# A state-space mixer with a routed expert layer: VectorE's routing through PSUM, another head and tail, and the expert tiles four units apart

## The chip, the cores and the metric

One core of a Trainium2 chip runs the whole program. The metric is the device time of one execution in microseconds. The kernel before took 2276.89 us in the median of three runs (2268.54 to 2281.24).

## What is computed

There are 16 sequences ("batches" below) of 512 tokens with 512 channels, all float32:

```
xn = layernorm(x)
x_dbl = xn @ x_proj_w.T                    # 128 + 16 (B) + 16 (C) columns
delta = softplus(x_dbl[:, :128] @ dt_proj_w.T + dt_proj_b)
state[d,n] = exp(delta[d] * A[d,n]) * state[d,n] + delta[d] * B[n] * xn[d]   # along the 512 tokens
s[d] = sum over n of state[d,n] * C[n] + xn[d] * D[d]                        # n = 0..15
top = the 2 best of 8 experts by xn @ gate_w + gate_b
f = mean over the two of relu(xn @ expert_w[e] + expert_b[e])
out = x + s * silu(f)
```

## The kernel before

**Units.** Channels lie on the 128 partitions, in four blocks (`dt`), and each of the 16 states `n` of a block is one unit: 64 units for a batch, called 0 to 63 here. A unit is one recurrence over 512 tokens. ScalarE makes the decay (`da_unit`, exp into one of three PSUM banks of `scan_ps`), GpSimd the input term for two units at once (`dbx_pair`, up to four pairs ahead), and VectorE runs the recurrence as one scan (`scan`). Then the state is multiplied by C: in most units by VectorE (`times_c`, into `p_sb`), in the last one or two units of a quad (four units) by GpSimd two quads later (`times_c_quad`, from `h_sb` into `pp_sb`). `POOL_C` says how many of a quad are GpSimd's; it is 20 of 64 in a batch. TensorE transposes each product and sums it in `y_ps` (`add_y`, `add_y_quad`), and ScalarE copies the sum of a channel block to `s_sb` (`copy_y`).

**The expert layer.** VectorE picks two experts for each token (`gate`) and works out a row for each of the 1024 choices, so that rows of one expert are together (`rank`). GpSimd scatters the tokens to those rows in DRAM (`scatter`), in 15 tiles of 128 rows. For each tile TensorE transposes the rows (`turn_rows`), multiplies by the weights of the tile's expert (`tile`), and ScalarE copies and rectifies (`keep_turned`, `tile_relu`). GpSimd gathers both rows of each token into `acc` with two indirect transfers (`gather_first`, `gather_second`, the second one adding). ScalarE then makes the sigmoid in three steps (`sigmoid`) and VectorE the output (`combine`), for the batch before, while the next one is being scanned.

**Order.** Each engine's order is written out: every engine runs the 64 units in turn, and tables say at which unit's place another piece of work stands. `STEPS` holds TensorE's projection steps (NT transposes xn, NX projects and gates, NK counts rows, NR and NS turn the results, Z0 to Z3 make delta; N is for the next batch); ScalarE follows `COPY_LAG` units later. `TILE_AT` holds the tiles, `SIG_AT` and `OUT_AT` sigmoid and combine, `FIRST_AT`, `SECOND_AT` and `SCATTER_AT` the quads at which GpSimd issues its indirect transfers. ScalarE stands at most three units ahead of VectorE, because it waits until a bank of `scan_ps` is free. Batches 0, 1, 14 and 15 are written out; a hardware loop of six turns does two batches a turn.

Of the kernel before, what the change touches and what calls it, by code (L numbers as in the profile page):

```python
# [54 lines left out]
FIRST_ROWS_AT = (5, 6)  # L55


def build(nc, x, xw, dw, db, alog, dpar, gw, gb, ew, eb, out):
# [14 lines left out]
    ND = [QUAD - c for c in POOL_C]  # L73
    DVE_C = sum(ND)

    ctx = ExitStack()
    with ctx:
# [45 lines left out]
        pool_pad = sb("pool_pad", [P, 5])  # L123
# [74 lines left out]
        row_sum = sem("row_sum")  # L198
        own_ready = sem("own_ready")
# [29 lines left out]

        def step_no(b, name):  # L230
# [21 lines left out]
        def quad_no(b, q):  # L252
            return b * QUADS + q
# [23 lines left out]
        def _(sp):  # L277
# [873 lines left out]
```

## Time and profile before

| | |
|---|---|
| median of three runs | 2276.89 us |
| the profiled execution | 2277.99 us, span 2276.2 us |
| VectorE busy | 1983.9 us, 87% |
| GpSimd busy | 1888.0 us, 83% |
| TensorE busy (matmul) | 1843.6 us, 81%; mean granted clock 0.93 of 2.4 GHz |
| ScalarE busy | 1378.6 us, 61% |
| transfers | 641 MB, 282 GB/s |

The profile was taken on one execution. A row of the order of time gives start, duration, engine, line, operation, output<-inputs and shape; in brackets how long the engine had been idle and what ended that. A row on waits gives who waited for whom, the total, how often, and the longest. PE is TensorE, DVE VectorE, ACT ScalarE, POOL GpSimd. Where several instructions of a kind stand in a row, they are one row with a count.

### The profile page before, as it was taken

How to read it: one execution, taken by the hardware profiler on the slowest of the kernel's cores; microseconds unless marked ns; L12 is line 12 of the kernel's file. 1: busy time of each engine (PE TensorE's matmuls, PEld its weight loads, DVE VectorE, ACT ScalarE, POOL GpSimd, SP SyncE). 2: the span in 40 equal slices, each digit the busy share in tenths (PEclk: the TensorE clock that was granted, in tenths of full speed). 3: DMA queues.
4: the chain of work that ended last, by engine and by line, in shares of the span. 5: the costliest groups of instructions: out<-in, count | busy, mean ns of one | idle time of the engine just before them, and what ended most of it. 6: DMA issues, size and time to landing. Idle time of an engine off the chain costs nothing.

```text
span 2276.2 us, 35000 instructions
## 1 busy us (share of the span) xinstructions
PE 1843.6 (81%) x8688; PEld 1192.7 (52%) x8688; DVE 1983.9 (87%) x3002; ACT 1378.6 (61%) x2370; POOL 1888.0 (83%) x1146
## 2 busy tenths in 40 slices
PE   2597988979788797888969888797987979888883
PEld 2364655546455564555546555465654646565552
DVE  3688898999889998899988989899888999989985
ACT  2465666666476665666656576565665666566663
POOL 2679889888888988889888988789888898898993
PEclk8698999989899998998989999899998999999997
DMA  5868798788968878798887978789797897987974
GB/s 212 291 229 336 238 345 279 266 323 256 365 199 308 310 259 327 232 327 290 262 309 240 367 245 295 278 258 367 222 323 258 267 352 228 360 269 265 337 253 127
DMA packets 281729, 641.47 MB, mean 282 GB/s; under 512 B 22529, under 2 KB 23041, under 8 KB 273297
## 3 DMA queue, kind: packets, MB, share of 16 engines
q1 hardware_dynamic: 187792, 445.84, 55.2%
q10 hardware_dynamic: 69120, 125.86, 15.6%
q0 software_dynamic: 24576, 67.13, 10.6%
q8 instruction: 83, 1.36, 0.2%
q14 instruction: 158, 1.29, 0.2%
HBM read 516.58 MB, written 122.16 MB: 281 GB/s over the span
## 4 chain that ended last, share of the span: by engine, by line
DVE 28%; PE 24%; issue 23%; POOL 12%; ACT 9%; ACTq 2%; DVEq 1%; DMA 1%; POOLq 0%; SPq 0%
PE z_ps L1028 12%; DVE scan_ps L881 7%; POOL dbx L444 6%; DVE p_sb L891 6%; DVE h_sb L881 4%; POOL xs_rows L470 4%; ACT scan_ps L597 3%; PE y_ps L1045 3%; PE proj_ps L980 2%; PE y_ps L1062 1%; POOL pp_sb L458 1%; DVE proj_ps L786 1%; PE proj_ps L972 1%; DVE stats L747 1%; PE xt_ps L1015 1%
## 5 line engine op out<-in xcount | busy, mean ns | idle before, releaser
L444 POOL TENSOR_TENSOR dbx<-b_sb,u_sb 128x1024 f32<-128x1024 f32 x512 | 1226.0, 2467 | 109.0 <-issue 41.1
L597 ACT ACTIVATE scan_ps<-delta,a_sb 128x512 f32<-128x512 f32 x1024 | 697.3, 688 | 645.2 <-DVE p_sb L891 612.2
L1028 PE MATMUL z_ps<-w_sb,xsT 128*128 128x512 f32 x1920 | 912.5, 620 | 111.1 <-ACT r_sb L618 111.0
L881 DVE TENSOR_TENSOR_SCAN scan_ps<-scan_ps,dbx 128x512 f32<-128x512 f32 x704 | 842.4, 1217 | 164.3 <-ACT scan_ps L597 138.6
L1028 PEld LDWEIGHTS z_ps<-w_sb,xsT 128*128 128x128 f32 x1920 | 360.8, 198 | 501.9 <-issue 501.5
L1045 PE MATMUL y_ps<-ident,p_sb 128*128 128x128 f32 x2816 | 430.3, 286 | 190.2 <-DVE p_sb L891 189.2
L458 POOL TENSOR_TENSOR pp_sb<-h_sb,c_sb 128x512 f32<-128x512 f32 (+1 forms) x256 | 404.9, 1582 | 163.1 <-PE y_ps L1062 143.8
L1045 PEld LDWEIGHTS y_ps<-ident,p_sb 128*128 128x128 f32 x2816 | 341.6, 146 | 354.4 <-DVE p_sb L891 238.3
L891 DVE TENSOR_TENSOR p_sb<-scan_ps,c_sb 128x512 f32<-128x512 f32 x704 | 473.4, 673 | 0.0
L881 DVE TENSOR_TENSOR_SCAN h_sb<-scan_ps,dbx 128x512 f32<-128x512 f32 x320 | 387.3, 1210 | 3.3 <-ACT scan_ps L597 3.2
L1030 PE MATMUL z_ps<-eb_sb,expert_hot 128*128 128x512 f32 x240 | 190.9, 796 | 0.0
L1062 PE MATMUL y_ps<-ident,pp_sb 128*128 128x128 f32 x1280 | 184.2, 275 | 1.1 <-POOL pp_sb L458 1.1
L1015 PE MATMUL xt_ps<-ident,xs 128*128 128x128 f32 x960 | 149.1, 279 | 20.2 <-ACT xsT L612 19.1
L470 POOL DMA_INDIRECT xs_rows<-xn,row_u x128 | 126.9, 992 | 36.7 <-issue 36.2
L618 ACT ACTIVATE r_sb<-z_ps 128x512 f32<-128x512 f32 x240 | 139.9, 583 | 23.9 <-PE z_ps L1030 23.9
L1062 PEld LDWEIGHTS y_ps<-ident,pp_sb 128*128 128x128 f32 x1280 | 150.7, 143 | 1.3 <-POOL pp_sb L458 1.3
L612 ACT ACTIVATE xsT<-xt_ps 128x512 f32<-128x512 f32 x240 | 140.8, 587 | 5.6 <-PE xt_ps L1015 3.8
L1015 PEld LDWEIGHTS xt_ps<-ident,xs 128*128 128x128 f32 x960 | 114.7, 145 | 24.4 <-ACT xsT L612 17.5
L1006 PE MATMUL proj_ps<-dun,dw_sb 128*128 128x512 f32 x128 | 88.6, 782 | 31.0 <-ACT delta L578 30.3
L493 POOL DMA_INDIRECT acc<-ys_rows,row_u x64 | 100.3, 1567 | 15.0 <-issue 11.2
L605 ACT ACTIVATE s_sb<-y_ps 128x512 f32<-128x512 f32 x64 | 37.8, 590 | 113.6 <-PE y_ps L1062 104.9
L980 PE MATMUL proj_ps<-xwg_sb,xT 128*128 128x168 f32 x512 | 89.2, 318 | 1.3 <-ACT xT L541 0.8
(99 smaller groups left out, 1405.2 us busy)
## 6 DMA issues: line engine op xcount, KB each, us to landing
w_sb<-in_ew SPq DMA_DIRECT2D x240, 1024.0 KB
b_sb<-bc_rows SPq DMA_DIRECT2D x64, 1024.0 KB, 10.9
xs<-xs_rows ACTq DMA_DIRECT2D x240, 256.0 KB
ys_rows<-r_sb ACTq DMA_DIRECT2D x240, 256.0 KB
c_sb<-bc_rows SPq DMA_DIRECT2D x64, 768.0 KB, 14.7
xn<-in_x SPq DMA_DIRECT2D x16, 1024.0 KB, 15.7
c_sb<-bc_rows SPq DMA_DIRECT2D x64, 256.0 KB, 15.9
xo<-in_x SPq DMA_DIRECT2D x64, 256.0 KB
```

What stands on the lines that cost most here:

```text
L444: nc.gpsimd.tensor_tensor(dbx[:, k % DBX_PAIRS], b_sb[:, 2 * m:2 * m + 2, :], u_sb[:, dt % 2, :].unsqueeze(1).to_broadcast([P, 2, T]), ALU ...
L458: nc.gpsimd.tensor_tensor(pp_sb[:, q % 2, 0:POOL_C[q]], h_sb[:, q % 2, 0:POOL_C[q]], c_sb[:, n:n + POOL_C[q], :], ALU.mult).then_inc(pp_re ...
L470: nc.gpsimd.indirect_dma_start(xs_dram[par], bass.IndirectOffsetOnAxis(ap=row_u[:, par, blk:blk + 1], axis=0), xn[:, blk % TT, :], None).t ...
L597: nc.scalar.activation(scan_ps[:, j % DA_BANKS, :], delta[:, dt % 2, :], ACT.Exp, scale=a_sb[:, dt, n:n + 1]).then_inc(da_ready, 1)
L612: nc.scalar.activation(xsT[:, (par * TILES + i) % 2], xt_ps[:], ACT.Copy).then_inc(xst_ready, 1)
L881: nc.vector.tensor_tensor_scan(state, bank, dbx[:, j // 2 % DBX_PAIRS, r % 2, :], 0.0, ALU.mult, ALU.add).then_inc(scanned, 1)
L891: nc.vector.tensor_tensor(p_sb[:, dve_no(0, j) % D_SLOTS, :], scan_ps[:, j % DA_BANKS, :], c_sb[:, n, :], ALU.mult).then_inc(p_ready, 1)
L1015: last = nc.tensor.matmul(xt_ps[:, c, :], xs[:, slot, c * P:(c + 1) * P], ident[:], start=True, stop=True, is_transpose=True)
L1028: nc.tensor.matmul(z_ps[:], xsT[:, slot, c, :], w_sb[:, i % WRING, c, :], start=(c == 0), stop=False)
L1030: nc.tensor.matmul(z_ps[:], expert_hot[:, par, i:i + 1].to_broadcast([P, P]), eb_sb[:], start=False, stop=True).then_inc(z_done, 1)
L1045: last = nc.tensor.matmul(y[:, tt, :], p_sb[:, slot, tt * P:(tt + 1) * P], ident[:], start=(n == 0 and tt == 0), stop=False, is_transpose= ...
L1062: last = nc.tensor.matmul(y[:, tt, :], pp_sb[:, q % 2, i, tt * P:(tt + 1) * P], ident[:], start=False, stop=(q % NQ == NQ - 1 and i == POO ...
```

## The change

It does this:

- `POOL_C` becomes (2, 2, 1, 0) in every channel block. GpSimd has 20 units of a batch as before, in 12 instructions where there were 16, and none in the last quad of a block.
- The tiles stand exactly four units apart, from unit 5 (the sixth) to unit 61. In the first batch they stand at 14 to 61, in the last at 5 to 52.
- `copy_y` moves from units 28, 44, 60 and 12 to 24, 41, 56 and 8, and each sigmoid stands behind a copy, one step in a unit, in the bank just copied; the fourth block of tokens is combined a batch later.
- The gathers stand about one quad later, and so does the scatter; both are cut finer. In the last batch the first gather stands inside the batch.
- In `gate`, two instructions on 8x4 elements, both of whose inputs lie in SBUF, become eight on 9 elements with a scalar per partition. In `rank`, the tiles' experts and the row numbers are kept in PSUM in place of `expert_f` and `row_f`, and the bank is given back at the end.
- The first batch has tables of its own, so the layernorm statistics of the next batch stand at unit 11 instead of 2. Before the first unit, `gate` stands ahead of `delta_u`, and TensorE no longer waits for the expert bias.
- At unit 60 the three banks are taken in another order (`AGAIN`): the same bank twice in a row there, and not at the end of a batch. At the end each of the four output blocks has a bank of its own.

The core of the diff:

```
-STEPS = {2: "Z1", 9: "Z2", 16: "NT0", 18: "NT1", 20: "NT2", 22: "NT3", 24: "NX0", 26: "NX1", 28: "Z3",
-         35: "NK", 40: "NR", 41: "NS", 46: "NZ0"}
+STEPS = {0: "Z1", 9: "Z2", 16: "NT0", 18: "NT1", 20: "NT2", 22: "NT3", 24: "NX0", 26: "NX1", 28: "Z3",
+         35: "NK", 41: "NR", 42: "NS", 48: "NZ0"}
+FIRST_STEPS = {0: "Z1", 9: "Z2", 21: "NT0", 23: "NT1", 25: "NT2", 27: "NT3", 29: "NX0", 31: "NX1", 33: "Z3",
+               40: "NK", 45: "NR", 46: "NS", 50: "NZ0"}
-DVE_LAG = 6
+DVE_LAG = 7
-STATS_AT = 2
-APPLY_AT = 11
+FRONT = {"stats": (2, 3, 4, 5), "var": 5, "root": 8, "apply": (11, 13, 13, 15), "gate": 32, "rank": 38}
+FIRST_FRONT = {"stats": (11, 11, 12, 12), "var": 13, "root": 16, "apply": (19, 19, 20, 20), "gate": 37, "rank": 44}
-POOL_C = (1, 2, 1, 1, 1, 1, 1, 2, 2, 2, 1, 1, 1, 1, 1, 1)
+POOL_C = (2, 2, 1, 0)
-TILE_AT = {8 + (i * 36) // 10: i for i in range(TILES)}
+TILE_AT = {5 + 4 * i: i for i in range(TILES)}
+FIRST_TILE_AT = {14 + (i * 34) // 10: i for i in range(TILES)}
+LAST_TILE_AT = {5 + (i * 34) // 10: i for i in range(TILES)}
-SIG_AT = (28, 32, 44, 48)
-OUT_AT = (29, 32, 45, 48)
-FIRST_AT = {3: (0, 1), 4: (2, 3)}
-SECOND_AT = {5: (0, 1), 6: (2, 3)}
-SCATTER_AT = {10: (0, 1), 11: (2, 3, 4), 12: (5, 6, 7)}
-ROWS_AT = (57, 60)
+ROWS_AT = (61, 63)
+COPY_Y_AT = {24: 0, 41: 1, 56: 2, 8: 3}
+SIG_AT = ((27, 28, 29), (43, 44, 45), (57, 58, 59), (9, 11, 12))
+FIRST_AT = {4: (0, 1), 5: (2,), 6: (3,)}
+SECOND_AT = {6: (0,), 7: (1,), 8: (2, 3)}
+SCATTER_AT = {11: (0, 1, 2), 12: (3, 4, 5), 13: (6, 7)}
...
-                    if j % N == 12:
-                        if j >= N:
-                            copy_y(b, par, j // N - 1)
+                    if j in COPY_Y_AT:
+                        if COPY_Y_AT[j] < DT - 1:
+                            copy_y(b, par, COPY_Y_AT[j])
...
-                nc.vector.tensor_tensor(hot[:, :, 0:TT], iota[:, 0:E].unsqueeze(2).to_broadcast([P, E, TT]),
-                                        topf[:, :, 0].unsqueeze(1).to_broadcast([P, E, TT]),
-                                        ALU.is_equal)
...
+                for k in range(2):
+                    for tt in range(TT):
+                        last = nc.vector.tensor_scalar(hot[:, :, k * TT + tt], iota[:, 0:E + 1], topf[:, tt, k:k + 1], None,
+                                                       ALU.is_equal)
...
-                nc.vector.tensor_scalar(expert_f[:], expert_f[:], float(E - 1), None, ALU.min).then_inc(tiles_min, 1)
+                nc.vector.tensor_scalar(expert_of, expert_of, float(E - 1), None, ALU.min).then_inc(tiles_min, 1)
...
-            delta_u(0, 0, 0)
             gate(0)
+            delta_u(0, 0, 0)
...
-            pe.wait_ge(eb_step, 7)
```

On VectorE, ahead of the first unit, before (from the sum of softplus, `proj_ps<-proj_ps,u_sb`, through the gate):

```order
17 L786 TENSOR_TENSOR proj_ps<-proj_ps,u_sb 128x512
18 L789 TENSOR_TENSOR u_sb<-proj_ps,xT 128x512
19 L797 MEMSET pad 128x1
20 L799 MAX top<-tok 128x8 x4
21 L802 MEMSET pad 128x1
22 L804 MAX_INDEX topi<-top,tok 128x8 x4
23 L807 TENSOR_REDUCE topf<-topi 128x8
24 L809 TENSOR_TENSOR hot<-iota,topf 128x8x4
25 L812 TENSOR_TENSOR hot<-iota,topf 128x8x4
```

and now:

```order
17 L855 MEMSET pad 128x1
18 L857 MAX top<-tok 128x8 x4
19 L860 MEMSET pad 128x1
20 L862 MAX_INDEX topi<-top,tok 128x8 x4
21 L865 TENSOR_REDUCE topf<-topi 128x8
22 L870 TENSOR_SCALAR hot<-iota,topf 128x9 x8
23 L844 TENSOR_TENSOR proj_ps<-proj_ps,u_sb 128x512
24 L847 TENSOR_TENSOR u_sb<-proj_ps,xT 128x512
```

The gate has moved ahead of the two softplus instructions, and its last two instructions have become eight. In every later batch the gate's place among the units is the same as before.

On GpSimd, in the second batch, around the gathers, before (`dbx` is a pair's input term, `pp_sb` the product of a quad, L484 the first gather, L493 the second):

```order
60 L444 TENSOR_TENSOR dbx<-b_sb,u_sb 128x1024 x2
61 L458 TENSOR_TENSOR pp_sb<-h_sb,c_sb 128x1024
62 L482 TENSOR_TENSOR pool_pad<-ones 128x1
63 L484 DMA acc<-ys_rows,row_u 128x512 x2
64 L444 TENSOR_TENSOR dbx<-b_sb,u_sb 128x1024 x2
65 L458 TENSOR_TENSOR pp_sb<-h_sb,c_sb 128x512
66 L482 TENSOR_TENSOR pool_pad<-ones 128x1
67 L484 DMA acc<-ys_rows,row_u 128x512 x2
68 L444 TENSOR_TENSOR dbx<-b_sb,u_sb 128x1024 x2
69 L458 TENSOR_TENSOR pp_sb<-h_sb,c_sb 128x512
70 L491 TENSOR_TENSOR pool_pad<-ones 128x1
71 L493 DMA acc<-ys_rows,row_u 128x512 x2
```

and now, from the seventh quad (quad 6) on (L538 is the first gather, L547 the second):

```order
62 L501 TENSOR_TENSOR dbx<-b_sb,u_sb 128x1024 x2
63 L512 TENSOR_TENSOR pp_sb<-h_sb,c_sb 128x1024
64 L536 TENSOR_TENSOR pool_pad<-ones 128x1
65 L538 DMA acc<-ys_rows,row_u 128x512
66 L545 TENSOR_TENSOR pool_pad<-ones 128x1
67 L547 DMA acc<-ys_rows,row_u 128x512
68 L501 TENSOR_TENSOR dbx<-b_sb,u_sb 128x1024 x2
```

The second gather of the first tokens stood in quad 5 and stands now in quad 6, behind a product of two units and the last of the first gathers.

On ScalarE, in the second batch, around the first copy of a channel block (L605) and the sigmoid that follows it (L643), before:

```order
224 L597 ACTIVATE scan_ps<-delta,a_sb 128x512
225 L541 ACTIVATE xT<-proj_ps 128x512
226 L605 ACTIVATE s_sb<-y_ps 128x4x128
227 L643 ACTIVATE y_ps<-acc 128x512
228 L597 ACTIVATE scan_ps<-delta,a_sb 128x512
```

and now (L654 is the decay of one unit, L662 the copy, L701 the sigmoid's first step):

```order
217 L662 ACTIVATE s_sb<-y_ps 128x4x128
218 L654 ACTIVATE scan_ps<-delta,a_sb 128x512
219 L691 DMA ys_rows<-r_sb 128x512
220 L654 ACTIVATE scan_ps<-delta,a_sb 128x512
221 L683 DMA xs<-xs_rows 128x512
222 L598 ACTIVATE xT<-proj_ps 128x512
223 L669 ACTIVATE xsT<-xt_ps 128x512
224 L654 ACTIVATE scan_ps<-delta,a_sb 128x512
225 L701 ACTIVATE y_ps<-acc 128x512
226 L654 ACTIVATE scan_ps<-delta,a_sb 128x512
```

The copy has moved from unit 28 to 24, and the sigmoid's first step from 28 to 27.

## Rows read from the trace of the kernel before

**Rows 1.** The page: busy time, share and instructions of each engine

```profile
PE 1843.6 (81%) x8688; PEld 1192.7 (52%) x8688; DVE 1983.9 (87%) x3002; ACT 1378.6 (61%) x2370; POOL 1888.0 (83%) x1146
```

**Rows 2.** Waits over the whole span: who waited for whom, total, times, longest

```profile
DVE scan_ps L881 <- ACT scan_ps L597: 138.6, 91, 4.9
...
DVE scan_ps L881 <- POOL dbx L444: 24.3, 16, 3.3
...
ACT s_sb L605 <- PE y_ps L1062: 104.9, 31, 5.6
```

**Rows 3.** Order of time in one steady batch: ScalarE and VectorE at units 28 and 60

```profile
1495.36 0.60 ACT L605 ACTIVATE s_sb<-y_ps 128x512 f32<-128x512 f32 x1 [2.84 <-PE y_ps L1062]
...
1497.45 1.23 DVE L881 TENSOR_TENSOR_SCAN scan_ps<-scan_ps,dbx 128x512 f32<-128x512 f32 x1 [2.88 <-ACT scan_ps L597]
...
1569.90 2.34 DVE L881 TENSOR_TENSOR_SCAN scan_ps<-scan_ps,dbx 128x512 f32<-128x512 f32 x2 [2.93 <-ACT scan_ps L597]
```

**Rows 4.** The same view where the hardware loop turns

```profile
1440.78 2.35 DVE L881 TENSOR_TENSOR_SCAN scan_ps<-scan_ps,dbx 128x512 f32<-128x512 f32 x2 [4.70 <-ACT scan_ps L597]
```

**Rows 5.** Order of time on VectorE: one scan and the next, a product between

```profile
2229.59 1.22 DVE L881 TENSOR_TENSOR_SCAN scan_ps<-scan_ps,dbx 128x512 f32<-128x512 f32 x1
...
2231.31 1.21 DVE L881 TENSOR_TENSOR_SCAN h_sb<-scan_ps,dbx 128x512 f32<-128x512 f32 x1
```

**Rows 6.** Order of time at the gate of one batch, VectorE and GpSimd

```profile
541.69 2.34 DVE L812 TENSOR_TENSOR hot<-iota,topf 128x32 f32<-128x32 f32 x1
...
541.61 4.70 POOL L444 TENSOR_TENSOR dbx<-b_sb,u_sb 128x1024 f32<-128x1024 f32 x2
```

**Rows 7.** Four small instructions in a row on VectorE, with a scalar per partition

```profile
90.34 0.58 DVE L773 TENSOR_SCALAR rstd<-newt,rstd 128x1 f32<-128x1 f32 x4
```

**Rows 8.** Lines 855 and 859: duration in ns, lowest, median, highest

```profile
L855 DVE TENSOR_SCALAR expert_f<-expert_f x16: 166/166/2172, 50.4 to 2070.8; 128x15 f32<-128x15 f32 x16
...
L859 DVE CAST expert_u<-expert_f x16: 160/164/2245, 52.6 to 2071.1; 128x15 uint32<-128x15 f32 x16
```

**Rows 9.** Order of time at the start of the program

```profile
12.34 2.93 ACT L533 ACTIVATE xn<-xn,shift,rstd 128x512 f32<-128x512 f32 x4 [2.48 <-DVE shift L778]
...
18.23 1.08 PE L972 MATMUL proj_ps<-ident,xn 128*128 128x128 f32 x4 [18.23 <-DVE eb_sb L925]
...
43.39 0.60 ACT L578 ACTIVATE delta<-proj_ps 128x512 f32<-128x512 f32 x1 [1.49 <-DVE u_sb L789]
...
44.67 2.34 DVE L812 TENSOR_TENSOR hot<-iota,topf 128x32 f32<-128x32 f32 x1
...
55.27 2.34 DVE L881 TENSOR_TENSOR_SCAN scan_ps<-scan_ps,dbx 128x512 f32<-128x512 f32 x2
...
77.15 1.29 DVE L747 BATCH_NORM_STATS2 stats<-xn 128x6 f32<-128x512 f32 x2 [17.81 <-DMA xn<-in_x]
```

**Rows 10.** The chain that ended last, at the start: start, length, what

```profile
64.97 6.63 DMA xs_rows<-xn,row_u
...
71.67 5.45 DMA xn<-in_x
```

**Rows 11.** Order of time on GpSimd: a first and a second gather

```profile
1461.82 0.97 POOL L484 DMA_INDIRECT acc<-ys_rows,row_u  x1 [0.30 <-issue]
...
1481.86 1.57 POOL L493 DMA_INDIRECT acc<-ys_rows,row_u  x1 [0.31 <-issue]
```

**Rows 12.** The end: VectorE's last product, and the chain's gathers, first and second

```profile
2239.99 0.67 DVE L891 TENSOR_TENSOR p_sb<-scan_ps,c_sb 128x512 f32<-128x512 f32 x1
...
2247.39 3.77 DMA acc<-ys_rows,row_u
...
2251.96 4.97 DMA acc<-ys_rows,row_u
```

**Rows 13.** TensorE: a slow tile, and ten microseconds around it (clock third from last)

```profile
1420.67 6.60 PE L1028 MATMUL z_ps<-w_sb,xsT 128*128 128x512 f32 x8 [1.95 <-ACT r_sb L618]
...
1418.00:1428.00 10.00, 8.05 (x22) 3.97 (x21) 7.55 (x9) 3.30 (x6) 7.49 (x4) 0.66 1.02 412
```

More of the change, by code:

```diff
@@ L72, in build @@
     CONST_P = CONST + E + 4
-    ND = [QUAD - c for c in POOL_C]
+    ND = [QUAD - POOL_C[q % NQ] for q in range(QUADS)]
     DVE_C = sum(ND)
+    POOL_QUADS = [q for q in range(QUADS) if POOL_C[q % NQ]]
+    PQ = len(POOL_QUADS) // DT
     ctx = ExitStack()
@@ L228, in is_first, with is_second @@
             return isinstance(b, int) and b == 0
+        def is_second(b):
+            return isinstance(b, int) and b == 1
         def step_no(b, name):
@@ L252, in quad_no, with z_in_y, z_buf @@
         def quad_no(b, q):
-            return b * QUADS + q
+            return b * len(POOL_QUADS) + POOL_QUADS.index(q)
+        def z_in_y(b, tt):
+            return not is_last(b) and not (isinstance(b, int) and b == B - 2 and tt >= 2)
+        def z_buf(b, tt):
+            if is_last(b):
+                return (proj_ps[:], xt_ps[:].rearrange("p c q -> p (c q)"), z_ps[:],
+                        y_ps[:, 0].rearrange("p t q -> p (t q)"))[tt]
+            if not z_in_y(b, tt):
+                return proj_ps[:]
+            return y_ps[:, tt % 2].rearrange("p t q -> p (t q)")
         def pair_no(b, k):
@@ L740, in _ @@
                 for part in range(3):
-                    sigmoid(B - 1, tt, B * DT, part)
+                    sigmoid(B - 1, tt, part)
         @block.vector
@@ L1059, in add_y_quad @@
                 pe.wait_ge(pp_ready, quad_no(b, q) + 1)
-                for i in range(POOL_C[q]):
+                for i in range(QUAD - ND[q]):
                     for tt in range(TT):
-                        last = nc.tensor.matmul(y[:, tt, :], pp_sb[:, q % 2, i, tt * P:(tt + 1) * P], ident[:],
-                                                start=False, stop=(q % NQ == NQ - 1 and i == POOL_C[q] - 1),
+                        last = nc.tensor.matmul(y[:, tt, :],
+                                                pp_sb[:, POOL_QUADS.index(q) % 2, i, tt * P:(tt + 1) * P], ident[:],
+                                                start=False, stop=(q % NQ == PQ - 1 and i == QUAD - ND[q] - 1),
                                                 is_transpose=True, skip_group_check=True)
@@ L1095, in batch @@
                         dt_proj(int(name[1]), step_no(b, name))
-                    if j + TURN_LEAD in TILE_AT:
-                        turn_rows(b, par, pair, TILE_AT[j + TURN_LEAD])
-                    if j in TILE_AT:
-                        tile(b, par, TILE_AT[j])
+                    if j + TURN_LEAD in tiles:
+                        turn_rows(b, par, pair, tiles[j + TURN_LEAD])
+                    if j in tiles:
+                        tile(b, par, tiles[j])
                     if on_dve(j):
@@ L1103, in batch @@
                         q = j // QUAD - 2
-                        if q >= 0:
+                        if q in POOL_QUADS:
                             add_y_quad(b, q)
-                        elif not is_first(b):
+                        elif q + QUADS in POOL_QUADS and not is_first(b):
                             add_y_quad(b - 1, q + QUADS)
```

300 lines of the change are left out of this document (169 added, 131 removed).

## The prediction

> **What bounds the kernel now.** I read the busy times first: VectorE is busy for 87% of the span, GpSimd for 83% [rows 1]. Both hand on to each other every unit, so neither is the plain bound; what counts is where VectorE stands still. It is idle for 2276.2 - 1983.9 = 292 us. The waits say on whom: 138.6 us on ScalarE's decays, 24.3 on GpSimd's input terms [rows 2]. The order of time says where, and it repeats from batch to batch. At unit 28 VectorE stands 2.9 to 3.3 us for a decay that ScalarE makes late, because ScalarE itself sat in front of a copy of `y_ps` until TensorE had finished [rows 3]; there are 14 such stalls, 44.6 us. At unit 60 the same: 16 stalls of 1.2 to 4.2 us, 42.2 us. Five of 4.6 to 4.9 us, 23.6 us, stand where the loop turns [rows 4]. The rest of the 138.6 is some 55 waits under 0.9 us, 25 us, and four of the first batch. ScalarE's own wait for the copies is 104.9 us [rows 2], which fits. Outside the steady part lie the start (first scan at 55.27, then 17.81 us for the next batch's x [rows 9]) and the end: from the end of the last product at 2240.66 [rows 12] to 2276.2 are 35.5 us.
>
> **The scale.** Scan and product take 1.72 us together (from 2229.59 to 2231.31 [rows 5]), a scan alone half of two, 1.12 (from rows 3, 2.34 with an overlap). 44 of one and 20 of the other are 98 us a batch before and after: `POOL_C` changes no count on VectorE. A GpSimd product of two units has the shape of a pair's input term, half of 4.70 [rows 6], one of one unit half of that; 20 units are 20 units, so I cost the new pattern at nothing. Its sum stays under the same cover: GpSimd's heavy quads come two quads after the heavy ones of `POOL_C`, when VectorE has its long quads. If that cover goes, the price is more of the 24.3 us.
>
> **Start: -10.** TensorE's first transposes wait until 18.23 for the expert bias [rows 9], though the normalised rows are ready at 12.34 + 2.93 = 15.3: -3.0. The gate in front of softplus lets the row count follow the copy of delta (ends at 43.39 + 0.60 = 43.99) instead of the gate, which ends at 44.67 + 2.34 = 47.0 [rows 9]: -3. In `rank` two instructions took 2172 and 2245 ns against medians of 166 and 164 [rows 8]: -4.1. In PSUM I take them at the median. That is 10.
>
> **First batch: -9.** The 17.81 us go, as the statistics move to unit 11. Late next: the eight scatter instructions still stand behind four input pairs. The last scatter instruction starts some 4 us earlier than at 64.97 [rows 10], at 60.8 (its pairs could run up to that much sooner), so the fifth pair is there at 60.8 + 1.0 + 2.3 = 64, while VectorE, with 12.8 us of work from a start at 45.3, wants it at 58: 6 back. The scatter lands 6.63 us after that start and x 5.45 later [rows 10], near 72.9, unit 11 is reached near 70: 3 back.
>
> **Gate: -18.** The instruction on 8x4 elements takes 2.34 us though its elements would take a tenth; it began 0.08 us after a GpSimd instruction and ended when the first of that pair did [rows 6]. It did so in 15 batches. Eight small ones at 0.58/4 = 0.15 us [rows 7] are 1.2: 15 x 1.2 = 18. The row used has one element, not nine. If each of the eight waits for GpSimd too, the cost is the last rival below; the other end is that they cost 0.8 less than I say.
> The Trainium skill ("SBUF — State Buffer", section on who interferes with whom) says that a VectorE instruction with two SBUF inputs and one in a two-port mode wait for a whole GpSimd instruction; "VectorE: DVE Perf Modes", on what auto-detection checks, gives that mode to a one-source instruction whose outermost sizes are even or equal. By that rule the removed instruction waits, as the trace has it, but the new ones (9 and 9, all in SBUF) would also. No row here shows such an instruction with nine elements. By that page the term of the gate would have the other sign.
>
> **Copies: -32 and -45.** The copy for units 0 to 15 moves from 28 to 24, and what it waits for from TensorE's place 22 to 18, ahead of NT2, NT3 and a tile: the place 28 has to wait behind the projection, 24 has not. I take all 44.6. The copy at 60 moves to 56 and needs place 50, with one tile (49) in front of it where there were two (51 and 54). With a tile at the low clock (6.60 us [rows 13]) it is just in time, so I take three quarters of 42.2, 32. Bounds: 0 and 42.
>
> **A new wait: +41.** Sigmoid's first step moves to unit 27 and needs the second gather, which moves from quad 5 to quad 6. GpSimd can't start the second pair of quad 6 before scan 19 has ended (four pairs ahead). From there: pair 2.33 (half of 4.70 [rows 6]), product of two units 2.35, a first gather with its guard 0.35 + 1.27 [rows 11], a guard 0.35, then 4.97 until the second gather lands [rows 12], sigmoid's step 0.54, decay and hand-over 0.84: 13.0 us. (The guard's 0.35 and the last two are from the same order of time.) VectorE gets from the end of scan 19 to the start of scan 27 in 10.1 (four times 1.72, three times 1.12 for the units that are GpSimd's or follow one). The stall is 2.9, in 14 batches 41 us. Bounds: with 3.77 us, the first gather's landing [rows 12], 1.7 x 14 = 24; nothing, if it lands in 2 us; with ScalarE blocked for longer under full transfer queues, 60. I take the row of the same instruction. Queued behind it on ScalarE are three decays and a tile's evacuation, and VectorE waits for these. While it stands, TensorE catches up with the projection (NX at 24 and 26), whose cost I therefore leave at nothing; without it TensorE has 32 us of work against 28 in units 16 to 31 and costs up to 1 us.
>
> **Tiles, small waits: -8.** Tiles four apart find the relu of the tile before done: TensorE's wait for it (1.95 in [rows 13]) shrinks. VectorE sees that only through the small waits. ScalarE's four densest units hold 7.6 us of work instead of 9.2. I take a third of 25.
>
> **End: -18.** The first gather (four at 1.27, landing 3.77) leaves the end, the four second ones (1.57 + 0.31 each [rows 11]) begin about 1 us after the last product instead of 11, and the four outputs no longer take turns for a bank; four combines of 2.1 in a row stay. That leaves 18 of 35.5. Bounds 10 and 22.
>
> **Unchanged.** 23.6 us at the loop's turns: VectorE's own jump; moving the shared bank to 60 doesn't take that away. 24.3 for GpSimd: the scatter is a quad later and as dense. SP's queue has new waits in front of weight loads, but each load has more than ten units until its tile.
>
> **The sum.** -10 - 9 - 18 - 32 - 45 + 41 - 8 - 18 = -99. 2277.99 - 99 = 2179; the median of the runs is 1.1 lower than the profiled execution, so 2178.
>
> **Rivals.**
> *The gathers are in time* (30%): the new wait isn't there. For it: GpSimd has waited for TensorE in that place and may not now; against: the pairs' limit is hard. 2178 - 41 + 3 for the projection = 2140.
> *TensorE stays late* (17%): the clock was at 0.66 of full, between its levels of 2.4 and 1.2 GHz, for 10 us around unit 50, after TensorE had waited twice for a relu, and a tile took 6.60 instead of 3.67 [rows 13]. Evenly spread tiles mean more short pauses. Then the copy at 56 keeps its 32 us, the small waits stay (8), and the projection costs 1 us in 14 batches: 2178 + 32 + 8 + 14 = 2232 at most, 2222 with some overlap. The Trainium skill ("TensorE: Matmul & The Clock Gate", second failure mode) warns that short pauses between groups of matmuls throw the clock back and forth. Rows 13 agree that it fell without one long pause; the same page would have this rival as its forecast.
> *The gate still waits for GpSimd* (7%): slower than before. Each of the eight instructions can let one GpSimd instruction in. With no scan done meanwhile, GpSimd runs dry after its four pairs, so four times 2.33, 9.3 us in place of 1.2, 15 x 8.1 = 122: 2300. It decides from three GpSimd instructions a gate on: (2277 - 2178)/15 = 6.6 us. For it: line 855, 15 elements in and out, waited once [rows 8]. Against: it did so only in the first batch.
> *The change does little* (4%): stalls only move, start and end gain half; about 2265.
> The forecast itself has 42%, between 2160 and 2200.
>
> **How the numbers follow.** Eight in ten: below, the gathers in time and the copies all gained, 2112; above, TensorE late, 2235. The two last rivals lie outside. About 0.5%, 11 us, is what a measurement here can tell from no change. Faster by more: 0.42 + 0.30 + 0.17 and a little of the rest, 0.90; within it 0.04; slower 0.06.
>
> **What would show it.** Right: VectorE's first scan near 45 us; no wait for x over 4 us; eight gate instructions near 0.2 us; ScalarE's wait for `y_ps` copies under 30 us in total; a wait of ScalarE's first sigmoid step for `acc` some 14 times, with VectorE idle 2 to 4 us at unit 27; 17 us from last product to end. Wrong: gate instructions of 2 us; copies still waiting 3 us; no wait for `acc`; a mean clock well under 0.93.

## The result

The changed kernel takes 2354.88 us in the median (2352.11 to 2357.44, four runs), the kernel before beside it 2278.41 (four runs): a ratio of 1.0345, 95% interval 1.0315 to 1.0374. It is slower by 3.4%, where the prediction had 2178 us and faster. The execution profiled below took 2356.41 us, its span is 2354.6. Two single executions of the experiments ran over 1.5% above the fastest of their own kernel (one of 2253.88 us in experiment 7, one of 3269.78 in experiment 8); they are left out of the ratios, but not of the medians.

### The profile page after: what moved, and what is told of

It is laid out like the page before. It is cut to its first block, busy times and chain, and to the rows that moved or that the text cites. A ratio compares the mean times of both kernels' runs of the same rounds, so it can differ in the third digit from the quotient of the medians.

```text
span 2354.6 us, 34705 instructions
## 1 busy us (share of the span) xinstructions
PE 1884.7 (80%) x8688; PEld 1244.5 (53%) x8688; DVE 1960.0 (83%) x3114; ACT 1374.4 (58%) x2370; POOL 1882.5 (80%) x1112
## 3 DMA queue, kind: packets, MB, share of 16 engines
q0 software_dynamic: 24576, 67.13, 10.7%
## 4 chain that ended last, share of the span: by engine, by line
PE 22%; issue 20%; DVE 19%; DMA 16%; POOL 14%; ACT 6%; SPq 2%; ACTq 1%; DVEq 1%; POOLq 0%
PE z_ps L1102 10%; POOL dbx L501 8%; DVE scan_ps L944 6%; DMA c_sb<-bc_rows 6%; PE proj_ps L1052 5%; DVE p_sb L954 4%; DMA xn<-in_x 4%; DVE h_sb L944 4%; DMA acc<-ys_rows,row_u 4%; PE y_ps L1118 3%; POOL pp_sb L512 3%; ACT scan_ps L654 2%; POOL acc L538 2%; DMA ys_rows<-r_sb 1%; PE proj_ps L1055 1%
## 5 line engine op out<-in xcount | busy, mean ns | idle before, releaser
L1102 PE MATMUL z_ps<-w_sb,xsT 128*128 128x512 f32 x1920 | 932.5, 631 | 78.6 <-ACT r_sb L675 78.4
L654 ACT ACTIVATE scan_ps<-delta,a_sb 128x512 f32<-128x512 f32 x1024 | 698.9, 690 | 457.6 <-DVE p_sb L954 423.5
L1102 PEld LDWEIGHTS z_ps<-w_sb,xsT 128*128 128x128 f32 x1920 | 372.8, 205 | 479.1 <-issue 455.1
L512 POOL TENSOR_TENSOR pp_sb<-h_sb,c_sb 128x1024 f32<-128x1024 f32 (+1 forms) x192 | 400.8, 2087 | 269.9 <-PE y_ps L1135 182.1
L1118 PEld LDWEIGHTS y_ps<-ident,p_sb 128*128 128x128 f32 x2816 | 342.4, 146 | 325.5 <-DVE p_sb L954 228.2
L1052 PE MATMUL proj_ps<-xwg_sb,xT 128*128 128x168 f32 x512 | 121.6, 397 | 126.8 <-ACT xT L598 126.1
L1135 PE MATMUL y_ps<-ident,pp_sb 128*128 128x128 f32 x1280 | 175.3, 277 | 0.0
L1052 PEld LDWEIGHTS proj_ps<-xwg_sb,xT 128*128 128x128 f32 x512 | 102.8, 252 | 131.6 <-ACT xT L598 128.7
L1087 PE MATMUL xt_ps<-ident,xs 128*128 128x128 f32 x960 | 162.4, 297 | 2.4 <-ACT xsT L669 1.2
L1087 PEld LDWEIGHTS xt_ps<-ident,xs 128*128 128x128 f32 x960 | 128.1, 155 | 17.5 <-issue 15.3
L701 ACT ACTIVATE y_ps<-acc 128x512 f32<-128x512 f32 x59 | 35.1, 595 | 144.7 <-DMA acc<-ys_rows,row_u 112.0
L547 POOL DMA_INDIRECT acc<-ys_rows,row_u x64 | 101.1, 1580 | 12.8 <-issue 11.9
```

The source lines that it names most:

```text
L512: nc.gpsimd.tensor_tensor(pp_sb[:, slot, 0:c], h_sb[:, slot, 0:c], c_sb[:, n:n + c, :], ALU.mult).then_inc(pp_ready, 1)
L654: nc.scalar.activation(scan_ps[:, bank_of(j), :], delta[:, dt % 2, :], ACT.Exp, scale=a_sb[:, dt, n:n + 1]).then_inc(da_ready, 1)
L1052: last = nc.tensor.matmul(proj_ps[:, (tt % 2) * PROJ:(tt % 2 + 1) * PROJ], xT[:, par, c, tt * P:(tt + 1) * P], xwg_sb[:, c, :], start=(c = ...
L1087: last = nc.tensor.matmul(xt_ps[:, c, :], xs[:, slot, c * P:(c + 1) * P], ident[:], start=True, stop=True, is_transpose=True)
L1102: nc.tensor.matmul(z_ps[:], xsT[:, slot, c, :], w_sb[:, i % WRING, c, :], start=(c == 0), stop=False)
L1118: last = nc.tensor.matmul(y[:, tt, :], p_sb[:, slot, tt * P:(tt + 1) * P], ident[:], start=(n == 0 and tt == 0), stop=False, is_transpose= ...
```

## The profile after

The first line of the page, to be held against [rows 1]:

```profile
PE 1884.7 (80%) x8688; PEld 1244.5 (53%) x8688; DVE 1960.0 (83%) x3114; ACT 1374.4 (58%) x2370; POOL 1882.5 (80%) x1112
```

VectorE has 24 us less to do than before and stands still for 2354.6 - 1960.0 = 394.6 us, 102 more. ScalarE and GpSimd are no busier than before either; TensorE is, by 41 us, at a mean granted clock of 0.90 where it was 0.93. The time went into VectorE's waits. Who waited for whom, to be held against [rows 2]:

```profile
DVE h_sb L944 <- ACT scan_ps L654: 143.5, 35, 10.7
DVE scan_ps L944 <- ACT scan_ps L654: 131.0, 73, 4.1
PE proj_ps L1052 <- ACT xT L598: 126.1, 15, 11.3
ACT y_ps L701 <- DMA acc<-ys_rows,row_u: 112.0, 12, 11.9
ACT tok L603 <- PE xt_ps L1087: 77.8, 15, 6.0
ACT tok L603 <- PE proj_ps L1055: 71.6, 17, 6.0
ACT s_sb L662 <- PE y_ps L1135: 9.8, 3, 7.3
```

The last line is the prediction's success: the copies of `y_ps` wait for 9.8 us in total instead of 104.9. The four above it are its failure. Read in order of time in one batch (start, duration, and in brackets idle time and releaser), they are one chain:

```profile
1682.51 0.71 ACT L654 ACTIVATE scan_ps<-delta,a_sb 128x512 f32<-128x512 f32 x1
1694.13 0.60 ACT L701 ACTIVATE y_ps<-acc 128x512 f32<-128x512 f32 x1 [10.90 <-DMA acc<-ys_rows,row_u]
1694.66 0.67 ACT L654 ACTIVATE scan_ps<-delta,a_sb 128x512 f32<-128x512 f32 x1
1695.28 0.58 ACT L598 ACTIVATE xT<-proj_ps 128x512 f32<-128x512 f32 x1
...
1703.07 0.45 ACT L603 ACTIVATE tok<-proj_ps 128x336 f32<-128x336 f32 x1 [4.54 <-PE xt_ps L1087]
...
1709.77 0.45 ACT L603 ACTIVATE tok<-proj_ps 128x336 f32<-128x336 f32 x1 [3.97 <-PE proj_ps L1055]
```

```profile
1695.90 2.61 PE L1052 MATMUL proj_ps<-xwg_sb,xT 128*128 128x168 f32 x8 [10.31 <-ACT xT L598]
...
1706.46 1.31 PE L1052 MATMUL proj_ps<-xwg_sb,xT 128*128 128x168 f32 x8
```

```profile
1695.46 1.22 DVE L944 TENSOR_TENSOR_SCAN h_sb<-scan_ps,dbx 128x512 f32<-128x512 f32 x1 [9.66 <-ACT scan_ps L654]
1704.71 1.23 DVE L944 TENSOR_TENSOR_SCAN scan_ps<-scan_ps,dbx 128x512 f32<-128x512 f32 x1 [2.05 <-ACT scan_ps L654]
1711.41 1.23 DVE L944 TENSOR_TENSOR_SCAN scan_ps<-scan_ps,dbx 128x512 f32<-128x512 f32 x1 [3.17 <-ACT scan_ps L654]
```

At unit 27 ScalarE stands in front of the sigmoid's first step for the second gather. Behind it in its queue is the copy of the last transposed x (`xT`, unit 28). TensorE's projection step NX0 needs that copy, waits 10.31 us, and comes back at half speed: the same eight matmuls take 2.61 us and, ten microseconds later, 1.31. The granted clock (third from last in a row: busy times of the engines, clock, share of the DMA engines, GB/s) was full ahead of the wait, and 0.71 of full, between its two levels of 1.2 and 2.4 GHz, in the stretch behind it:

```profile
1672.00:1684.00 12.00, 11.54 (x58) 7.42 (x58) 11.59 (x14) 9.21 (x16) 11.82 (x8) 1.00 0.88 277
1684.00:1696.00 12.00, 1.69 (x12) 1.12 (x10) 2.34 (x4) 1.87 (x4) 11.53 (x10) 0.77 0.64 201
1696.00:1704.00 8.00, 8.00 (x32) 6.54 (x33) 6.18 (x8) 3.46 (x8) 5.85 (x3) 0.71 0.35 70
```

Then ScalarE waits for it twice more, at the copies of `tok`, and VectorE each time behind ScalarE. Why the gather is late is on GpSimd (first VectorE's scan 19, on which GpSimd's limit of four pairs rests):

```profile
1673.87 1.21 DVE L944 TENSOR_TENSOR_SCAN h_sb<-scan_ps,dbx 128x512 f32<-128x512 f32 x1
...
1676.68 0.19 POOL L536 TENSOR_TENSOR pool_pad<-ones 128x1 f32<-128x1 f32 x1
1677.02 1.00 POOL L538 DMA_INDIRECT acc<-ys_rows,row_u  x1 [0.15 <-issue]
1678.03 4.71 POOL L501 TENSOR_TENSOR dbx<-b_sb,u_sb 128x1024 f32<-128x1024 f32 x2
1682.66 2.40 POOL L512 TENSOR_TENSOR pp_sb<-h_sb,c_sb 128x1024 f32<-128x1024 f32 x1
...
1686.71 1.59 POOL L547 DMA_INDIRECT acc<-ys_rows,row_u  x1 [0.15 <-issue]
```

The last of these rows is the second gather. It is issued at 1686.71 and lands at 1694.1, 7.4 us later.

I counted VectorE's idle times (of 0.3 us or more) by the unit at which they stand. In microseconds over all batches:

| place | before | after |
|---|---|---|
| units 27, 28 | 51 | 124, in 15 batches |
| units 29 to 32 | 15 | 90 |
| units 52, 59, 60 | 61 | 2 |
| where the loop turns | 24 | 18 |
| units 5, 6, behind the loop's turn | 0 | 30, in 5 batches |

The gate, to be held against [rows 6]. Its eight instructions stand beside GpSimd's indirect gathers and not beside a pair:

```profile
1427.13 1.59 POOL L547 DMA_INDIRECT acc<-ys_rows,row_u  x1 [0.15 <-issue]
...
1428.11 1.17 DVE L870 TENSOR_SCALAR hot<-iota,topf 128x9 f32<-128x9 f32 x8
...
1429.03 1.57 POOL L547 DMA_INDIRECT acc<-ys_rows,row_u  x1 [0.31 <-issue]
...
1430.04 9.92 POOL L501 TENSOR_TENSOR dbx<-b_sb,u_sb 128x1024 f32<-128x1024 f32 x4
```

The start and the end, beside [rows 9] and [rows 12]:

```profile
45.84 2.34 DVE L944 TENSOR_TENSOR_SCAN scan_ps<-scan_ps,dbx 128x512 f32<-128x512 f32 x2
...
64.64 2.35 DVE L944 TENSOR_TENSOR_SCAN scan_ps<-scan_ps,dbx 128x512 f32<-128x512 f32 x2 [6.06 <-POOL dbx L501]
...
77.18 1.29 DVE L805 BATCH_NORM_STATS2 stats<-xn 128x6 f32<-128x512 f32 x2 [6.71 <-DMA xn<-in_x]
...
2333.99 1.27 DVE L954 TENSOR_TENSOR p_sb<-scan_ps,c_sb 128x512 f32<-128x512 f32 x2
```

The loss behind the loop's turn was in no term of the sum. In order of time, ScalarE and TensorE, then VectorE:

```profile
1489.58 0.60 ACT L675 ACTIVATE r_sb<-z_ps 128x512 f32<-128x512 f32 x1 [4.70 <-issue]
...
1490.32 6.42 PE L1102 MATMUL z_ps<-w_sb,xsT 128*128 128x512 f32 x8 [5.45 <-ACT r_sb L675]
...
1503.44 2.07 PE L1078 MATMUL proj_ps<-dun,dw_sb 128*128 128x512 f32 x2 [4.29 <-issue]
...
1507.77 0.69 ACT L624 ACTIVATE u_sb<-proj_ps,db_sb 128x512 f32<-128x512 f32 x1 [8.30 <-PE xt_ps L1087]
...
1510.29 1.22 DVE L944 TENSOR_TENSOR_SCAN h_sb<-scan_ps,dbx 128x512 f32<-128x512 f32 x1 [6.04 <-ACT scan_ps L654]
```

ScalarE turns (4.70), then makes the relu of the last tile but one, now at unit 0. TensorE has waited for it with its last tile (unit 61), does that slowly (6.42), and only then turns itself (4.29). The two turns stand one behind the other.

## The experiments

Each is the changed kernel with the edit shown, where nothing else is said. Every ratio is to the kernel before, run on the same chip, with its 95% interval.

**1. The sigmoid one unit later**

```
-SIG_AT = ((27, 28, 29), ...
+SIG_AT = ((28, 29, 30), ...
```

> The changed kernel with the first tokens' sigmoid one unit later (units 28, 29, 30), so that the copy of the last transposed x (`xT`, place 28) stands ahead of it on ScalarE. Theory A (the wait for the gather holds up that copy, TensorE's projection waits for the copy and is late for the two copies of `tok`): the stalls at units 29 to 32, some 90 us in 14 batches, go, and the one at 27 or 28 (124 us) shrinks by one unit each, 14 x 1.7 = 24: 2355 - 90 - 24 = about 2240. Theory B (TensorE is late by itself, from the evenly spaced tiles and its clock): only the 24 us, about 2330.

Measured: 2304.65 us, 1.0100 (1.0079 to 1.0121). VectorE's idle time fell by 94 us, to 2314.7 - 2014.5 = 300.2, and of the 90 us at units 29 to 32 some 5 were left, with 9 us of new ones just behind unit 38. But it was busy 54 us longer: in 10 of 16 batches the gate took 5 to 7 us instead of 1.2. So theory A held for the stalls, and the gate took more than half of that back. The time lies between the two figures that were expected, and neither of them had the gate.

**2. The copy one unit earlier, the sigmoid where it is.** The edit moves TensorE's five steps NT0 to NX0 one unit ahead; ScalarE's copies follow them.

```
-STEPS = {..., 16: "NT0", 18: "NT1", 20: "NT2", 22: "NT3", 24: "NX0", ...
+STEPS = {..., 15: "NT0", 17: "NT1", 19: "NT2", 21: "NT3", 23: "NX0", ...
```

> The changed kernel with TensorE's steps NT0 to NT3 and NX0 one unit earlier (15, 17, 19, 21, 23); gather and sigmoid stay. The copy of NT3 falls on unit 27, where it stands ahead of the sigmoid on ScalarE. Queue theory (TensorE is held only because that copy is queued behind the sigmoid's wait): VectorE's stall at 27 stays, some 124 us, and the 90 us at 29 to 32 go: 2355 - 90 = 2265, plus up to 14 x 5.5 = 77 if the gate leaves the gathers' side. Rival (the stalls at 29 to 32 come from the length of the wait itself, or from TensorE's load of work): 124 and 90 stay, 2355.

Measured: 2338.88 us, 1.0269 (1.0226 to 1.0313). Its waits, against 126.1 and 77.8 + 71.6 above:

```profile
PE proj_ps L1052 <- ACT xT L598: 0.8, 1, 0.8
...
ACT tok L603 <- PE proj_ps L1055: 23.4, 17, 6.3
```

At units 29 to 32 some 3 us of the 90 are left. The wait itself didn't stay whole: the stalls at unit 27 fell from 124 us to 87, while those at unit 24 rose from 12 to 33. But a wait that is shorter by a third doesn't take stalls from 90 us to 3; the order of the queue does. VectorE's idle time fell by 84 us, its busy time rose by 71: the gate took 6.9 to 7.0 us in 12 batches. The time is near what had been expected for that case, 2265 + 77 = 2342. In one batch, in order of time:

```profile
1272.63 6.93 DVE L870 TENSOR_SCALAR hot<-iota,topf 128x9 f32<-128x9 f32 x8
1272.89 1.55 POOL L547 DMA_INDIRECT acc<-ys_rows,row_u  x1 [0.31 <-issue]
1273.87 5.26 POOL L501 TENSOR_TENSOR dbx<-b_sb,u_sb 128x1024 f32<-128x1024 f32 x2
```

One of the eight took 6.0 us of it. It had begun 0.7 us ahead of the first input term, while the gather was being issued, and it ended with the second input term. So a gather beside the gate is no shelter when a pair follows close behind.

**3. The second gather of the first tokens one quad earlier**

```
-SECOND_AT = {6: (0,), 7: (1,), 8: (2, 3)}
+SECOND_AT = {5: (0,), 7: (1,), 8: (2, 3)}
```

> The changed kernel with the second gather of the first tokens one quad earlier on GpSimd, in quad 5, behind the first gather of the third tokens. The sigmoid and everything else stay. Theory A: the data lands at about the time ScalarE asks for it; of some 213 us of VectorE's stalls at units 27 to 32 at most 30 stay: 2355 - 185 = 2170 (2155 to 2200). Theory B: what TensorE is late by stays, 90 of the 213 us and the rest of its slowness: 2230 or more.

Measured: 2241.06 us, 0.9833 (0.9817 to 0.9850). One gather's place turns 3.4% slower into 1.7% faster, 114 us. Theory A's 2170 is missed; theory B's "2230 or more" holds, though not its 90 us: at units 29 to 32 some 59 us are left. So this run alone doesn't decide between the two. ScalarE still waited 28 us for the data, with the copy behind it, and TensorE 30 for the copy:

```profile
PE proj_ps L1052 <- ACT xT L598: 30.0, 12, 4.3
ACT y_ps L701 <- DMA acc<-ys_rows,row_u: 28.2, 7, 4.9
```

**4. The new gate alone, in the kernel before.** The edit is that of the diff shown above.

> The kernel before with nothing but the new gate: eight instructions on nine elements in place of two on 8x4. By the prediction's term: 15 x 1.2 = 18 us less, 2260 (ratio 0.992). Rival: the time saved on VectorE is given back as a longer wait for GpSimd or ScalarE, ratio 1.000.

Measured: 2361.06 us, 1.0341 (1.0314 to 1.0369): 81 us slower, by eight small instructions. In order of time, VectorE and GpSimd:

```profile
1275.64 7.70 DVE L811 TENSOR_SCALAR hot<-iota,topf 128x9 f32<-128x9 f32 x8
1275.67 4.67 POOL L444 TENSOR_TENSOR dbx<-b_sb,u_sb 128x1024 f32<-128x1024 f32 x2
1280.70 2.34 POOL L458 TENSOR_TENSOR pp_sb<-h_sb,c_sb 128x1024 f32<-128x1024 f32 x1 [0.36 <-PE y_ps L1061]
```

The gate ends 0.3 us after the third GpSimd instruction. Not all eight waited: in this gate three took 2.4 us each, as long as a GpSimd instruction, and five took 0.22. Over all gates (duration in ns, lowest, median, highest):

```profile
L811 DVE TENSOR_SCALAR hot<-iota,topf x128: 220/223/2420, 50.0 to 2137.9; 128x9 f32<-128x9 f32 x128
```

The gate took 7.7 us in 14 of 16 batches. VectorE's busy time rose by 73 us. Both of my expectations were wrong here. The prediction's own rival, which had 7%, had the mechanism, with four GpSimd instructions a gate where there were three. The rule quoted in the prediction from the Trainium skill ("SBUF — State Buffer", who interferes with whom; "VectorE: DVE Perf Modes", auto-detection) says just that these instructions wait too, and this run agrees (2.4 us for an instruction that takes 0.22 undisturbed).

**5. The old gate in the changed kernel**, with two instructions on 8x4:

```
+nc.vector.tensor_tensor(hot[:, 0:E, k * TT:(k + 1) * TT], iota[:, 0:E]..., topf[:, :, k]..., ALU.is_equal)
```

> The changed kernel with the old gate: two instructions on 8x4 elements. In the changed kernel the gate stands beside GpSimd's indirect gathers, in the kernel before beside a pair of input terms. Theory D (an instruction of either form waits for a whole GpSimd instruction on tensors, and not for an indirect transfer; the eight small ones wait three times, the old one once): here nothing is there to wait for, the two take 0.5 us in place of 1.2, so 0 to 11 us less than the changed kernel, 2343 to 2355. Theory E (the new form is the cheaper one, as the prediction has it): 18 us more, 2373.

Measured: 2347.12 us, 1.0308 (1.0267 to 1.0348). The two take 0.29 us together and the eight 1.17. 2373 is excluded; whether the old form is faster here can't be told, as the intervals overlap. This fits theory D, and what freed the gate in the changed kernel is its neighbour: both forms are short in 15 of 16 batches. The neighbour is there because the change puts second gathers into quads 7 and 8, and the gate stands at unit 32. Whether they meet depends on how far GpSimd is ahead, as experiments 1 and 2 show.

**6. Gather in quad 5 and sigmoid at 29 to 31, with the new gate and with the old** (below, the latter is the repaired kernel)

```
+SECOND_AT = {5: (0,), 7: (1,), 8: (2, 3)}
+SIG_AT = ((29, 30, 31), ...
```

> The changed kernel with the second gather of the first tokens in quad 5 and their sigmoid at units 29, 30, 31. The gather lands before ScalarE asks, and the copy of `xT` stands ahead. Theory A: the stalls that are left in units 24 to 32 (106 us when only the gather is moved) fall to some 25, TensorE doesn't wait for the copy: 2241 - 80 = 2160 if the gate is not delayed. Theory D on top of it: with the stalls gone the gate stands beside pairs again and takes 7 us in place of 1.2 in most batches, 14 x 5.5 = 77 back: about 2235. If TensorE is late by itself (theory B), the stalls at 30 to 32 stay: 2215 or more with a gate of 1.2.

> As the kernel with the second gather in quad 5 and the sigmoid at 29 to 31, but with the old gate of two instructions on 8x4. Theory D: the gate takes 2.6 us where a pair runs beside it and 0.5 where none does: 2160 to 2190, and clearly less than with the new gate if that one is delayed. Theory E: slower than with the new gate by 18 us.

Measured: 2203.01 us, 0.9653 (0.9620 to 0.9686), and 2198.65, 0.9648 (0.9614 to 0.9683). ScalarE waits 0.5 us for the gather and TensorE 11.0 for the copy in the second. The stalls at units 29 to 32 are 20 and 22 us, where the changed kernel had 90 and the kernel before 15: so much at most can be TensorE's own lateness (theory B), once neither the wait nor the queue stands in its way. Theory A's 2160 is missed by 43 us; it had 25 us left at units 24 to 32, and 66 and 67 are. The gate stayed beside the gathers in both, so the loss that theory D feared didn't come; the two forms can't be told apart by time, though the old one is shorter (0.3 to 1.0 against 1.2 to 1.8 us in all batches but one). What now leads VectorE's waits is GpSimd:

```profile
DVE scan_ps L944 <- POOL dbx L501: 87.1, 48, 6.0
```

**7. The tiles one unit earlier**, `TILE_AT = {4 + 4 * i ...}`, alone and with the gather in quad 5

> The changed kernel with the tiles at units 4, 8, ... 60 in place of 5, 9, ... 61, so that the relu of the last tile but one stands at unit 63, ahead of the loop's turn, and not at unit 0 behind it. Theory C (where the loop turns, the last tile on TensorE waits for a relu that stands behind ScalarE's turn, TensorE's own turn comes after that tile, and ScalarE then waits for TensorE at unit 6): the six stalls of 6 us at units 5 to 8 go, 2355 - 30 to 36 = 2320 to 2325. Rival (these stalls come from the loads of b and c or from Z1 at place 0): no change, 2355.

> The changed kernel with the second gather in quad 5 and the tiles at 4, 8, ... 60. Theory C: the six stalls of 6 us at units 6 to 8 go (37 us): 2241 - 37 = 2205, if the rest of the stalls stays. Rival: moving the tiles by one unit makes the projection's copies as late as it makes them early elsewhere (with the tiles alone only 17 of the 36 us came back): 2225 to 2241.

Measured: 2337.72 us, 1.0244 (1.0196 to 1.0292), and 2235.96, 0.9779 (0.9715 to 0.9844). The first is some 17 us under the changed kernel, between the two figures expected: the five stalls behind the loop's turn fell from 6.0 us each to 3.7, and two gates of 7 us took part of the gain back. With the gather moved, the tiles give nothing that can be told from experiment 3, as the rival had it.

**8. What stands behind the loop's turn.** The repaired kernel with the last five tiles one unit earlier, with Z1 at unit 2, with all tiles earlier, and two pairs of these.

```
-TILE_AT = {5 + 4 * i: i for i in range(TILES)}
+TILE_AT = {5 + 4 * i - (i >= 10): i for i in range(TILES)}
-STEPS = {0: "Z1", ...
+STEPS = {2: "Z1", ...
```

> The changed kernel with the second gather in quad 5, the sigmoid at 29 to 31 and the old gate (2199 us, called the repaired kernel), and the last five tiles one unit earlier (44, 48, 52, 56, 60), the first ten where they are. The relu of the last tile but one stands at unit 63, ahead of the loop's turn. Theory C: the five stalls of 5 to 6 us at units 3 to 5 go (26 us): 2173. Rival (they come from something else at the loop's turn): 2199.

> The repaired kernel with TensorE's step Z1 at unit 2 in place of 0, as in the kernel before, and its copy at 8 in place of 6. Theory C (TensorE is late there because its last tile and its own turn follow ScalarE's turn, and ScalarE stands at the load of rows at unit 6 whatever Z1 does): the stalls stay, 2199. Rival (Z1 at 0 is what is waited for): 26 us less, 2173.

> The repaired kernel with all tiles at 4, 8, ... 60. Theory C: the stalls at the loop's turn go as with the last five alone, and with the sigmoid behind the copy of `xT` the projection isn't pushed: 2173. Rival: the tiles at 24 and 28 stand in front of the projection's steps of the same units and cost there what they give back (70 us at units 28 and 29 were seen with the sigmoid at 27): 2200 to 2240.

> The repaired kernel (second gather in quad 5, sigmoid at 29 to 31, old gate) with the last five tiles one unit earlier and Z1 at unit 2. Each alone gave some 10 us at the loop's turn. If they cut the same stall: 2188, as with one. If each takes its own part (the tile behind the relu, and the projection step that TensorE begins with after its turn): 2178.

> The repaired kernel with all tiles at 4, 8, ... 60 and Z1 at unit 2. As above: 2187 if they cut the same stall, 2177 if each takes its own part.

Measured, in this order: 2189.99 us, 0.9638 (0.9595 to 0.9680); 2188.80, 0.9620 (0.9582 to 0.9659); 2187.39, 0.9614 (0.9576 to 0.9652); 2184.51, 0.9600 (0.9564 to 0.9637); 2184.29, 0.9599 (0.9555 to 0.9643). Against the repaired kernel's 0.9648 none of them stands clear by its interval. The traces say more: the five stalls of 4.6 to 5.7 us became 3.0 to 3.3 with the last tiles moved, 1.9 to 3.1 with Z1 moved, and 0.4 or less with both. So both things had a part, and my theory C, by which Z1's place was nothing, was half wrong. But with Z1 at 2 there are new stalls of 0.6 to 1.2 us at unit 8 in 14 batches, some 12 us, which take back nearly half of the 26. The medians differ by 14 us, and the intervals of the two ratios overlap.

**9. The copies back at 28 and 60** in the repaired kernel; the sigmoid of the third tokens moves to 61 to 63 and the last batch's first one to 29 to 31 for that

```
-COPY_Y_AT = {24: 0, 41: 1, 56: 2, 8: 3}
+COPY_Y_AT = {28: 0, 41: 1, 60: 2, 8: 3}
```

> The repaired kernel with the copies of `y_ps` at 28 and 60 again, as in the kernel before (the sigmoid of the third tokens at 61 to 63 for that). If the copy's place was what gained (the prediction's 32 + 45 = 77 us): 2199 + 77 = 2276, with ScalarE waiting some 3 us in front of each. If it is `POOL_C`, whose last quad has no GpSimd product, so that the sum is complete at TensorE's place 18 already: no wait at 28 or 60, 2199.

Measured: 2200.22 us, 0.9670 (0.9631 to 0.9708), no difference; ScalarE waits for one copy in the whole run, the last. So the place to which the copy moved gained nothing. What is left as the cause is `POOL_C`: with no GpSimd product in a block's last quad the sum is complete on TensorE four units earlier. The kernel before with the new `POOL_C` alone was not run, so that it suffices without the other moves is argued.

The best version of the runs is that of experiment 8 with late tiles and Z1 both moved: 2184.51 us, 4.0% under the kernel before (0.9564 to 0.9637). Its span is 2181.3 us, VectorE's idle time 2181.3 - 1953.1 = 228.2. The version with all tiles and Z1 moved can't be told from it.

## Why the prediction was wrong

The sum had -99 us and the profiled executions differ by 2356.41 - 2277.99 = +78, so 177 us are missing. By its steps:

**A new wait (+41): here it failed, twice.** It was measured at 124 us at unit 27. One stall of 9.66 us shows what 2.9 lacked. First, I let GpSimd begin the second pair of quad 6 as soon as scan 19 had ended. In that batch scan 19 ended at 1675.1 and that pair began at 1680.4 (half of 4.71 behind 1678.03), since GpSimd came late from the pairs and the first gather of quad 5: 5.3 us. (In the 15 batches it was 1.8 to 6.7 us, and where it was 1.8 the stall was 3.7 to 4.4.) "20 units are 20 units" left out that the new pattern and the gathers fill these quads. Second, I took 4.97 us for the landing from the end of the program, where the DMA engines' share was 0.49 and 65 GB/s were moved; here it was 7.4, at 0.64 and 201 GB/s (5.3 to 8.9 over the 15 batches). Together 2.9 + 5.3 + 2.4 = 10.6, near enough to 9.66. (VectorE's own way of "10.1" is 10.2 by the terms given, four times 1.72 and three times 1.12.) The trace of before had it in the batches, from issue to landing:

```profile
DMA to landing us min/median/max: 4.9/8.6/10.4
```

That is line 493, all 64 second gathers of the kernel before. With its median the term would have been 14 x (2.9 + 3.6) = 91 us.

Then the sentence "Queued behind it on ScalarE are three decays and a tile's evacuation ... While it stands, TensorE catches up with the projection": the old order shown has the copy of `xT` at unit 28 ahead of the sigmoid, the tables leave it there, and the sigmoid's move to 27 puts it behind; the excerpt of the new order ended one line short of it. TensorE can't catch up on a projection whose input is behind the wait. That was 90 us at units 29 to 32. Experiment 2 puts the copy ahead of the wait, of which two thirds stay, and 3 us are left; experiment 3 takes away most of the wait and leaves the copy behind it, and 59 are left. So the rival "TensorE stays late" had the right engine and the wrong reason: it was held, and the clock fell with the wait (1.00 ahead of it, 0.77 in it, 0.71 behind it), not the other way round.

**Copies (-32 and -45): the size right, the reason half.** The stalls at 28, 52 and 60 fell from 112 us to 2 beside the new one. The term had two parts, the copy's new place and the sum that is ready earlier (place 18 in place of 22). By experiment 9 the first gained nothing; the second, which is `POOL_C`, is what is left.

**Gate (-18): measured -18.3** on VectorE (39.6 before, 21.3 after), and wrong all the same. The edit is worth +81 us where it was argued (experiment 4). It came out right by luck: the gathers had moved beside the gate, which I had not seen. The rival's break-even was near the mark: it had 6.6 us over the 1.2 of an undisturbed gate, and the gates of experiment 4 took 6.5 over it. By its own prices that is more than three GpSimd instructions (3 x 2.33 - 1.2 = 5.8), not "from three on".

**Start (-10): right**, 55.27 to 45.84, with the first transposes at 15.58. **First batch (-9): -3**, from 149.5 us between the first scans of batches 0 and 1 to 146.3: the stall for the scatter's pair (6.06) came as said, that for x was 6.71 us and not 3, and ScalarE's delays of the later units grew, one of them to 3.7 us. **End (-18): -16**, from the end of the last product at 2335.3 to 2354.6 are 19.3 us.

**Unchanged, 23.6 us at the loop's turns: wrong** by 30 - 5 = +25. The tile at 61 and the relu at unit 0 put TensorE's turn behind ScalarE's. I had looked at VectorE's own jump alone.

The failed steps are 124 + 90 - 41 = 173 us of the new wait and 25 at the loop, 198 of the 177. Against them stand the small stalls at units 30 and 52 of before, 12 and 18 us, which went with the copies where I had counted 8. What is left about cancels: 10 us more at unit 24, 6 in the first batch and 2 at the end, against 16 that the copies gave beyond their terms.

Of the signs named ahead, the first scan (45.84), the gate's instructions and ScalarE's wait for the copies (9.8 us) came; the wait for x was over 4 us, the stall at unit 27 was 3.7 to 10.7 us where 2 to 4 were expected, and the mean clock was 0.90.

## What to carry to other kernels

When a wait is added on an in-order engine, list what is queued behind it up to the point where the next engine is fed, not up to the next unit of work: the wait's own stall was 124 us here, its queue another 90. Take a transfer's landing time from the same neighbourhood, not from a quiet end. And price an instruction that can be held by another engine by what stands beside it: the same edit was worth +81 us in one kernel and nothing that could be measured in the other, and whatever moves the neighbours changes its price, as experiments 1 and 2 did.

## What the runs showed of the hardware

An instruction on 128x9 elements in SBUF with a scalar per partition was held on VectorE for a whole GpSimd instruction on tensors: of a row of eight, three took 2.4 us each and five 0.22 (7.70 us together, experiment 4). Beside GpSimd's indirect DMAs alone eight took 1.17 us, between two of 1.6. Where a pair followed such a DMA at once, a single one took 6.0 us: it began 0.7 us ahead of the pair and ended with it, in 12 batches of experiment 2. What held it in those 0.7 us the traces don't show.

The instructions of `rank` that had once taken 2172 and 2245 ns [rows 8] never took over 180 with their input in PSUM, though in 15 of 16 batches both began while a GpSimd instruction on tensors was running:

```profile
L915 DVE TENSOR_SCALAR proj_ps<-proj_ps x16: 177/177/180, 44.8 to 2157.2; 128x15 f32<-128x15 f32 x16
L919 DVE CAST expert_u<-proj_ps x16: 161/163/164, 45.0 to 2157.5; 128x15 uint32<-128x15 f32 x16
```

An accumulating gather of 128 rows took 4.9 to 10.4 us to land in the kernel before, a plain one of the same size 3.3 to 7.4.
